# One core: the attention stage's four-tile loops written out as one straight program of 64 tiles

## The reference, cut to what matters

```python
# L0_attn_x: (8, 1024, 256); 16 heads of 16; segments of 64 tokens
mod = (silu(c) @ wmod).reshape(8, 6, 1, -1)
h = layernorm(x) * (1 + ca) + sa
x = x + ga * infini_attention(h)              # with @ W_o.T
h = layernorm(x) * (1 + cb) + sb
x = x + gb * moe(h)                           # 8 experts, top 2

# infini_attention, for each segment of 64 tokens, carrying M, z:
A_mem = sigma(q) @ M / (sigma(q) . z + EPS)
A_dot = softmax(causal(q @ k.T / sqrt(dk))) @ v
A_s = beta * A_mem + (1 - beta) * A_dot
V_prev = sigma(k) @ M / (sigma(k) . z + EPS)
M, z = M + sigma(k).T @ (v - V_prev), z + sigma(k).sum(-2)
```

## Time and profile before

| what | us |
|---|---|
| median of 3 runs | 1519.62 (1515.5 to 1525.3) |
| time of the profiled execution | 1524.05 |
| its span, first to last instruction | 1522.2 |
| mean granted TensorE clock over the span | 0.903 of full speed |

### The profile page before, as it was taken

The page is one execution under the profiler, slowest core; times in us unless marked ns, Lnnn a source line. Parts: engine busy times, 40 slices in busy tenths (PEclk is TensorE's granted clock), DMA queues, the critical chain, the costliest instruction groups (busy, mean ns, idle before and its releaser), DMA issues. The chain is left out here.

```text
span 1522.2 us, 58123 instructions
## 1 busy us (share of the span) xinstructions
PE 1272.6 (84%) x19297; PEld 911.9 (60%) x19299; DVE 1104.0 (73%) x3310; ACT 700.3 (46%) x1373; POOL 901.1 (59%) x982
## 2 busy tenths in 40 slices
PE   4599989888888889888324599999999999999995
PEld 0377767766666677666101266666666666666663
DVE  2489888777778788777499666677767667767763
ACT  2278878776677778677431022222222222222221
POOL 2169988777778888779310155555555555555553
PEclk8599999999899999899555599999999999999998
DMA  9612332223232333224551144444444444444441
GB/s 224 139 51 57 90 85 77 75 71 79 64 81 76 84 83 78 73 72 106 192 151 59 35 82 85 82 86 86 86 80 84 82 84 83 84 80 86 83 79 27
DMA packets 114694, 131.62 MB, mean 86 GB/s; under 512 B 16762, under 2 KB 94658, under 8 KB 114386
## 3 DMA queue, kind: packets, MB, share of 16 engines
q0 software_dynamic: 31200, 54.91, 19.4%
q1 hardware_dynamic: 83314, 74.02, 18.5%
HBM read 61.49 MB, written 43.12 MB: 69 GB/s over the span
## 5 line engine op out<-in xcount | busy, mean ns | idle before, releaser
L1335 PE MATMUL psum<-w13s,xT 128*128 x1620 | 373.6, 380 | 11.8 <-issue 10.9
L1406 POOL DMA_INDIRECT out<-yo,si x135 | 215.3, 1595 | 246.3 <-DVE si L1312 165.6
L1335 PEld LDWEIGHTS psum<-w13s,xT 128*128 128x128 f16 x1620 | 155.6, 98 | 175.7 <-issue 21.6
L1344 ACT ACTIVATE sg<-psum 128x512 f32<-128x512 f32 x135 | 80.6, 597 | 310.6 <-PE psum L1335 235.9
L1306 POOL DMA_INDIRECT grow<-moe_rows,gi x135 | 133.0, 985 | 148.1 <-DVE si L1312 99.8
L1383 PE MATMUL psum<-w2s,hT 128*128 x1620 | 199.0, 273 | 0.6 <-issue 0.6
L1383 PEld LDWEIGHTS psum<-w2s,hT 128*128 128x128 f16 x1620 | 152.7, 98 | 16.5 <-issue 1.1
L1357 ACT ACTIVATE hs<-hf 128x512 f16<-128x512 f32 x135 | 85.0, 629 | 167.4 <-DVE hf L1350 166.2
L1362 DVE TENSOR_TENSOR hs<-hf,hs 128x512 f16<-128x512 f32 x135 | 93.4, 692 | 93.9 <-ACT hs L1357 91.8
L692 POOL TENSOR_TENSOR pT<-sc,pT 128x1024 f16<-128x1024 f32 x64 | 136.4, 2131 | 10.9 <-ACT pT L687 10.9
L1376 DVE COPY hT<-psum 128x1024 f16<-128x1024 f16 x135 | 93.0, 689 | 37.7 <-PE psum L1369 31.2
(11 more groups left out here) (206 smaller groups left out, 2776.0 us busy)
## 6 DMA issues: line engine op xcount, KB each, us to landing
stk<-qk SPq DMA_DIRECT2D x384, 64.0 KB, 2.8
moe_rows<-hrows SPq DMA_DIRECT2D x128, 128.0 KB, 2.3
stage<-in_w SPq DMA_DIRECT2D x24, 512.0 KB, 5.2
out<-xall SPq DMA_DIRECT2D x128, 64.0 KB, 2.4
xall<-in_x SPq DMA_DIRECT2D x8, 896.0 KB, 18.0
grow<-moe_rows,gi POOLq DMA_INDIRECT x135
out<-yo,si POOLq DMA_INDIRECT x135, 3.8
wmod_sb<-in_wmod SPq DMA_DIRECT2D x1, 1536.0 KB
```

The costliest lines, as they stand in the source:

```text
L1335: i = k.e.matmul(bank[:, :], xT[:, k.b, a, c, :], w13s[:, b_, bass.ds(ex_reg * (G * 2 * I) + (c * 2 * I + at), I)], start=(c == 0 and (a, ...
L1406: k.e.indirect_dma_start(out_rows, bass.IndirectOffsetOnAxis(ap=si[:, k.j, :], axis=0), yo[:, k.j, :], None, bounds_check=B * T - 1, oob_i ...
```

## The change

The loops of all five engines are gone. `engine_program` writes NT + deepest slots out straight, with tile numbers that are always Python integers; wait values and addresses are constants, the offsets PRE and FIRST are dropped with the `sem_inc`s that put them there, and a wait for a tile before the first is left out. The short list of bank waits (`full`) is now used on PE from slot 13 on and until slot 63, where it was used in the loop. The order of the stages in a slot, the lags, the buffers and all computation stay. The source lines behind L434 move up by 7, later ones by up to 38.

```diff
...
-        def __init__(self, e, s, j):
-            self.e, self.s, self.j, self.b = e, s, j, j % 2
-            self.t = s * 4 + j
+        def __init__(self, e, t, full):
+            self.e, self.t, self.full = e, t, full
+            self.s, self.j, self.b = t // NJ, t % NJ, t % 2
 
         def when(self, stage, back=0):
 
-            if stage in PER_SEGMENT:
-                if isinstance(self.s, int):
-                    of = min(self.t - back, NT - 1) // NJ
-                    return S[stage], max(of, -1) + 1 + PRE
-                return S[stage], self.s + ((self.j - back) // NJ + 1 + PRE)
-            if isinstance(self.s, int):
-                of = min(self.t - back, NT - 1)
-                return S[stage], max(of, -1) + 1 + PRE
-            return S[stage], self.s * 4 + (self.j - back + 1 + PRE)
+            of = min(self.t - back, NT - 1)
+            return S[stage], (of // NJ if stage in PER_SEGMENT else of) + 1
...
             latest, others = BANK_FREE[name]
-            for stage, back in latest + (others if isinstance(self.s, int) else ()):
+            for stage, back in latest + (() if self.full else others):
                 self.wait(stage, back)
...
-            if not isinstance(self.s, int) or self.s > 0:
-                self.e.wait_ge(s_st[self.j], self.s * 32 + FIRST)
+            if self.s > 0:
+                self.e.wait_ge(s_st[self.j], self.s * 32)
 
         def of_tile(self, rows):
 
-            return rows[:, bass.ds(self.t, 1), :].rearrange("p o d -> p (o d)")
+            return rows[:, self.t, :]
...
         for b2, toks in enumerate(HALVES):
-            k.e.dma_start(out[2 * k.j + b2, bass.ds(k.s * SEG, SEG), :],
-                          xall[toks, bass.ds(k.t, 1), :].rearrange("p o d -> p (o d)")).then_inc(s_out, 16)
+            k.e.dma_start(out[2 * k.j + b2, k.s * SEG:(k.s + 1) * SEG, :],
+                          xall[toks, k.t, :]).then_inc(s_out, 16)
...
     def engine_program(name, e):
         stages = program[name]
         deepest = max(lag for lag, _ in stages)
-        periods = deepest // 4 + 1
...
-        for s in range(periods):
+        for i in range(NT + deepest):
+            full = deepest < i < NT
+            for lag, stage in stages:
+                if 0 <= i - lag < NT:
+                    stage(Tile(e, i - lag, full))
...
-        with e.Fori(periods, NS) as s:
-            for j in range(4):
-                slot(s, j)
-        for s in range(NS, NS + periods):
-            for j in range(4):
-                slot(s, j)
...
-        def start(name, e):
-            for n in names:
-                if owner[n] == name:
-                    e.sem_inc(S[n], PRE)
-            engine_program(name, e)
...
```

More of the change, by code:

```diff
@@ L408, in attention @@
     class Tile:
-        def __init__(self, e, s, j):
-            self.e, self.s, self.j, self.b = e, s, j, j % 2
-            self.t = s * 4 + j
+        def __init__(self, e, t, full):
+            self.e, self.t, self.full = e, t, full
+            self.s, self.j, self.b = t // NJ, t % NJ, t % 2
         def when(self, stage, back=0):
-            if stage in PER_SEGMENT:
-                if isinstance(self.s, int):
-                    of = min(self.t - back, NT - 1) // NJ
-                    return S[stage], max(of, -1) + 1 + PRE
-                return S[stage], self.s + ((self.j - back) // NJ + 1 + PRE)
-            if isinstance(self.s, int):
-                of = min(self.t - back, NT - 1)
-                return S[stage], max(of, -1) + 1 + PRE
-            return S[stage], self.s * 4 + (self.j - back + 1 + PRE)
+            of = min(self.t - back, NT - 1)
+            return S[stage], (of // NJ if stage in PER_SEGMENT else of) + 1
         def wait(self, stage, back=0):
-            if not isinstance(self.s, int) or self.t >= back:
+            if self.t >= back:
                 self.e.wait_ge(*self.when(stage, back))
@@ L433, in wait_banks @@
             latest, others = BANK_FREE[name]
-            for stage, back in latest + (others if isinstance(self.s, int) else ()):
+            for stage, back in latest + (() if self.full else others):
                 self.wait(stage, back)
         def wait_apart(self, *stages):
-            apart(self.e, passed, [self.when(*w) for w in stages])
+            apart(self.e, passed, [self.when(*w) for w in stages if self.t >= (w + (0,))[1]])
         def arrived(self, sems, n=1):
@@ L446, in arrived_before @@
             s, j = self.s + (self.j - back) // 4, (self.j - back) % 4
-            if not isinstance(s, int) or s >= 0:
+            if s >= 0:
                 self.e.wait_ge(sems[j], s * (16 * n) + 16 * n)
         def stored(self):
-            if not isinstance(self.s, int) or self.s > 0:
-                self.e.wait_ge(s_st[self.j], self.s * 32 + FIRST)
+            if self.s > 0:
+                self.e.wait_ge(s_st[self.j], self.s * 32)
         def of_tile(self, rows):
-            return rows[:, bass.ds(self.t, 1), :].rearrange("p o d -> p (o d)")
+            return rows[:, self.t, :]
     def done(ins, stage):
@@ L484, in store @@
         for b2, toks in enumerate(HALVES):
-            k.e.dma_start(rows_dram[bass.ds(k.s * SEG + (2 * k.j + b2) * T, SEG), 0:2 * D],
+            k.e.dma_start(rows_dram[(2 * k.j + b2) * T + k.s * SEG:(2 * k.j + b2) * T + (k.s + 1) * SEG, 0:2 * D],
                           hrows[toks, k.j, :].bitcast(F32)).then_inc(s_st[k.j], 16)
         for b2, toks in enumerate(HALVES):
-            k.e.dma_start(out[2 * k.j + b2, bass.ds(k.s * SEG, SEG), :],
-                          xall[toks, bass.ds(k.t, 1), :].rearrange("p o d -> p (o d)")).then_inc(s_out, 16)
+            k.e.dma_start(out[2 * k.j + b2, k.s * SEG:(k.s + 1) * SEG, :],
+                          xall[toks, k.t, :]).then_inc(s_out, 16)
     def stats(k):
-        k.e.wait_ge(s_x[k.j] if isinstance(k.s, int) and k.s < 2 else s_xx[k.j], 32)
+        k.e.wait_ge(s_x[k.j] if k.s < 2 else s_xx[k.j], 32)
         k.wait("aggr", 4)
@@ L937, in logit_copy @@
         k.wait("rtr")
-        done(k.e.activation(logits[:, :, bass.ds(k.t, 1)].rearrange("p e o -> p (e o)"), bkH[:, D:D + E], ACT.Copy,
+        done(k.e.activation(logits[:, :, k.t], bkH[:, D:D + E], ACT.Copy,
                                scale=1.0 / W_SCALE), "lg")
@@ L958, in engine_program @@
         deepest = max(lag for lag, _ in stages)
-        periods = deepest // 4 + 1
[L961 to L967, removed]
-        for s in range(periods):
-            for j in range(4):
-                slot(s, j)
-        with e.Fori(periods, NS) as s:
-            for j in range(4):
-                slot(s, j)
-        for s in range(NS, NS + periods):
[L976 to L986, removed]
-    with nc.Block() as block:
-        def start(name, e):
-            for n in names:
-                if owner[n] == name:
-                    e.sem_inc(S[n], PRE)
-            engine_program(name, e)
+        for i in range(NT + deepest):
[3 more added lines that the diff above has]
+                    stage(Tile(e, i - lag, full))
+    with nc.Block() as block:
         @block.sync
         def _(e):
+            engine_program("sync", e)
             for j in range(4):
[L998 to L1001, removed]
+                e.wait_ge(s_st[j], 32 * NS)
             e.wait_ge(s_out, 32 * NT)
@@ L1005, in _ @@
         def _(e):
-            start("tensor", e)
+            engine_program("tensor", e)
         @block.vector
         def _(e):
-            start("vector", e)
+            engine_program("vector", e)
         @block.scalar
         def _(e):
-            start("scalar", e)
+            engine_program("scalar", e)
         @block.gpsimd
         def _(e):
-            start("gpsimd", e)
+            engine_program("gpsimd", e)
 def experts(nc, ctx, sb_, sem_, banks, trib, iota, count, tok_id, out_rows, rows_dram,
```

## The result

The changed kernel takes 1439.6 us (median of 4, 1432.5 to 1441.8) against 1519.9 of the kernel before (1515.5 to 1525.3): ratio 0.946, 95% interval 0.942 to 0.951. The forecast was 1436.4, and the gain, 83.2 us forecast, is 80 us by the medians. So differences read between the two traces come out some 11 us larger in all than the difference of the medians.

What follows compares the result with a forecast made beforehand. PE's loop back branches in attention, stalling on instruction fetch, were taken as the bound. Terms of -81.7 us (tiles 10 to 61) and -1.5 us (block's start) gave -83.2, from 1519.62 to 1436.4 us; range 1418 to 1471.

Steps and rivals of the forecast that it cites:

- The bound: Attention, PE's loop: 11 back branches, each costing 3.9 us of idleness and 2.5 us of slow matmuls.
- The tile time: Attention tiles 10 to 61: 8.95 us each in straight code instead of 10.55, taking 81.7 us off.
- an occasional wait with a slow clock after it: Attention tiles: 0.10 us a tile added to 8.85 for `scores` sometimes waiting for its DMAs.
- a share of 11 us of waits: SP's attention loop: 11 of the 24.8 us that `scores` waits for `stk` go with the address and wait arithmetic.
- SP keeps the pace: Rival, attention: `stk` waits come from the DMAs themselves, so tiles stay at 9.58 us; 1468.5 us, chance 0.17.
- The start: Head of the attention block: dropping DVE's two dozen `sem_inc`s gains 1.5 us, between 0 and 2.4.
- Two parts that the sum had at nothing: Attention: bank waits in slots 13 to 15, pipeline drain and the other engines' longer program were among those put at nothing.
- 8.5 is a floor: Attention: with stalls gone, PE, DVE and POOL meet at 8.2 to 8.5 us busy per tile.
- what is late next: Attention: the chain of PE's `update`, `mem_mm`, DVE's long list and back has no slack; tiles settle at 8.85.
- The slower rival: Attention, PE's fetching can't keep up: 3.9 us exposed at each of some 97 packets, 1815 us; chance 0.015.
- The rival that a branch costs next to nothing: Attention, PE's back branches: the 3.9 us only covers another wait, or about 108 ns each; 1518 us, chance 0.015.
- Waits for `stk` well under 10 us: Sign of being right, attention: `scores` on PE would wait for `stk` well under 10 us.

Runs made afterwards that it cites:

- e3: Kernel before with all engines but PE written out straight, PE keeping its loop: 1503.6 us, 0.994 of the kernel before.
- e1: Kernel before with PE alone written out straight, the other four engines keeping their loops: 1448.8 us, 0.959 of the kernel before.
- e5: The changed kernel measured again without any edit, as yardstick: 1429.4 us, 0.946 of the kernel before.
- e4: Kernel before with all engines but SP written out straight, SP keeping its loop: 1453.0 us, 0.959 of the kernel before.
- e7: Kernel before with all five engines straight, but semaphore offsets and their sem_incs kept: 1431.6 us, 0.948 of the kernel before.
- e6: Kernel before with PE and SP straight, DVE, ACT and POOL keeping their loops: 1434.8 us, 0.950 of the kernel before.
- e8: The changed kernel with SP's list reordered to low, store, high: 1417.7 us, 0.940 of the kernel before.
- e11: The changed kernel with PE's expert-stage loop body lengthened from 8 to 32 slots: 1449.0 us, from a single execution.

## Why the prediction was right

**The bound.** It said that PE's loop, at 11 back branches, sets the attention stage, by 3.9 us of idleness and 2.5 us of slow matmuls each. Undone alone (e3) it brings back 71 us; done alone (e1) it gives 63 of the 81. The trace agrees in its parts: over the same 51 tiles the idleness at the back branches fell by 43.1 (forecast 43.1), PE's busy time by 461.19 - 433.89 = 27.3 (forecast 27.5), and the waits for `stk` by 24.8 - 10.0 = 14.8 (forecast 11). Their sum is 85.2; the other waits of PE grew a little, and the starts of `mem_mm` show 84.0, against 81.7. Part of this closeness is luck: the two traces differ by 91.7 us in their spans, and some 11 of these are there because a slower than median execution was profiled before and the quickest after. By the medians the gain is 80 on the first chip and 82 in e5, so the 83.2 was a little too much.

**The tile time.** 8.95 us forecast, 8.905 and 8.917 measured in two traces. The three straight tiles at 8.85 plus 0.10 for "an occasional wait with a slow clock after it" came out right. The waits come 14 times in 51 tiles, 10.0 us or 0.20 a tile, and only two of them have a slower `mem_mm` behind them; the 8.85 under them was on the high side.

**SP.** The step gave its address arithmetic a share of 11 us of waits. The mechanism stands, but its price alone is higher than this share: SP's loop costs 17 us with all others straight (e4 against e7) and 13 with PE straight (e1 against e6, 0.959 and 0.950). In e4 half of that is PE's busy time at the lower clock, in e1 none of it. The rival "SP keeps the pace" was wrong with 9.58; with SP's loop left in, it is 9.35 (e4) or 9.17 (e1). Its core was right all the same: the DMAs' own order still cost 10 us of waits, and e8 took them away.

**The start.** 1.5 us forecast between 0 and 2.4, 2.05 measured, and shown by e7 to be the `sem_inc`s. Two parts that the sum had at nothing were not quite nothing: from DVE's first statistics to tile 10 took 98.45 us before (147.90 - 49.45) and 95.88 after (143.04 - 47.16), and from tile 61 to the next block 61.37 (747.45 - 686.08) and 62.64 (659.85 - 597.21). They nearly cancel.

**The floor.** "8.5 is a floor" and what is late next, DVE's chain through `update` and `mem_mm`: in e8 the tile takes 8.65 us, and PE's wait is almost only at `update` (L752, 0.27 us, in 40 of 51 tiles). Its row ends by "issue", so the profile does not show whom it waits for; that it is DVE's chain is argued and not shown.

**Fetching.** The slower rival needed 0.86 us exposed per packet; no such gaps appear. Fewer packets came on q8 than before (130 against 149). The rival that a branch costs next to nothing is wrong for code that must be fetched again, and right for code that stays, as the expert loop and e11 show side by side.

**A miss.** "Waits for `stk` well under 10 us": they are 10.0 to 12.1. I took three tiles without a wait for the rule; the change's own first wait, at 151.57 us, falls just where that sample had been taken.

## What to carry to other kernels

Look for idleness with no releaser at the first instruction of a loop's body, count it against the passes, and compare the instruction packets of a pass with those of straight code: if a pass fetches its whole body, the loop saves no fetching, and each branch cost here its stall plus the slow clock behind it. Not every engine needs unrolling. Here PE's was worth 63 us and SP's another 13 to 17, while the loops of DVE, ACT and POOL cost 3 to 6 us together (0.5 us a pass on DVE), and nothing as long as PE was late. And where one queue issues both urgent and patient DMAs, put the patient ones where that queue waits anyway.

## What the runs showed of the hardware that was not expected

- Whether PE's branch stalls goes with the length of the body: the 8-slot body of the expert stage runs with no gap by "issue" of over 0.61 us and with 3 packets in 500 us; 32 slots of the same code stall 3.8 and 3.4 us and fetch 45; the attention body of 9 packets of 16 KB stalls 3.9 on average, twice that body 4.2. The Trainium skill (Runtime: NRT & Kernel Launch, Instruction fetch mechanics) gives the rule that a taken branch to a target outside the window of code that the engine holds has to wait for a DMA fetch. The two loops agree with it.
- A wait of 1.41 us was followed by a `mem_mm` of 1.50 us instead of 0.92, while twelve waits of 0.21 to 1.14 us in the same stretch left it at 0.92. In the stretches compared the granted clock was 0.92 (kernel before), 0.96 (e4), 0.99 (e1 and the change) and 1.00 (e8), with the same matmuls taking 461, 446, 434, 434 and 429 us. PE idled 77, 31, 34, 20 and 12 us in them, so the sum of the idleness does not decide it: e1 idled more than e4 and was granted more.
- The 22 `sem_inc`s at the head of DVE's block cost 2.05 us, to the hundredth the same in e7 against the change.
